# Four taps of q's convolution on VectorE, convolutions finished half by half, and ranks from a difference, in a MetaFormer block

## The reference, cut to what matters

```python
x = x + conv_attention(layernorm_over_channels(x))
t = tokens(x);  t = t + mixture_of_experts(layernorm(t));  return image(t)

# conv_attention, cut to its steps
qkv = einsum('bchw,oc->bohw', x, w_qkv) + b_qkv
qkv = max over 2x2 positions                     # 24 x 24 are left
qkv = 3x3 depthwise convolution(qkv, w_dw) + b_dw
q, k, v = split(qkv)                             # 8 heads of 12 channels
q, k = q / clip(norm(q), 1e-12), k / clip(norm(k), 1e-12)
attn = einsum('bhcn,bhdn->bhcd', q, k) * temperature
out = sum over kk in (6, 8, 9, 9) of a_i * (topk_softmax(attn, kk) @ v)
out = gelu(out), repeated 2x2;  return einsum(out, w_proj) + b_proj
```

## Time and profile before

| | us |
|---|---|
| median of 3 runs | 164.18 (162.23 to 167.53) |
| the profiled execution | 162.02 |
| its span, first to last instruction | 160.1 |
| TensorE busy | 141.9 (89% of the span) |
| VectorE busy | 126.3 (79%) |
| ScalarE busy | 83.9 (52%) |
| GpSimd busy | 70.6 (44%) |

### The profile page before, as it was taken

The page is one execution under the profiler, slowest core; times in us unless marked ns, Lnnn a source line. Parts: engine busy times, 40 slices in busy tenths (PEclk is TensorE's granted clock), DMA queues, the critical chain, the costliest instruction groups (busy, mean ns, idle before and its releaser), DMA issues.

```text
span 160.1 us, 2626 instructions
## 1 busy us (share of the span) xinstructions
PE 141.9 (89%) x812; PEld 120.1 (75%) x812; DVE 126.3 (79%) x321; ACT 83.9 (52%) x153; POOL 70.6 (44%) x63
## 2 busy tenths in 40 slices
PE   7918959999989898999799928999999999999970
PEld 2404839999979573878568917999999999999950
DVE  0999877999868398927734997499799989989982
ACT  3525795304063503666677630666576566676730
POOL 8999953692000000200000789064736736526461
PEclk9996999999999999999999996999999999999998
DMA  5799000000000000000000001001001001000101
GB/s 145 204 256 246 5 0 4 2 0 0 4 0 0 0 2 0 4 0 0 0 0 4 0 0 37 0 0 37 4 0 37 0 0 37 0 0 0 37 0 37
DMA packets 3749, 4.41 MB, mean 28 GB/s; under 512 B 1934, under 2 KB 3290, under 8 KB 3644
## 3 DMA queue, kind: packets, MB, share of 16 engines
q1 hardware_dynamic: 3338, 3.86, 9.6%
q10 hardware_dynamic: 402, 0.44, 0.8%
HBM read 3.42 MB, written 0.88 MB: 27 GB/s over the span
## 4 chain that ended last, share of the span: by engine, by line
PE 65%; DVE 21%; issue 5%; ACT 4%; DMA 2%; SPq 0%; DVEq 0%; ACTq 0%
PE psum L912 15%; PE psum L914 14%; PE psum L913 14%; PE psum L1076 3%; PE psum L954 3%; PE psum L949 3%; PE psum L950 3%; PE psum L1006 3%; DMA xT<-xt 2%; DVE xn_lo L624 2%; DVE yg L849 2%; DVE h_hi L636 2%; DVE stats L697 2%; PE psum L1049 2%; PE psum L887 1%
## 5 line engine op out<-in xcount | busy, mean ns | idle before, releaser
L425 POOL TENSOR_TENSOR xs<-xs,yg 96x384 f32<-96x384 f32 x23 | 31.3, 1360 | 51.2 <-DVE yg L852 26.8
L638 DVE TENSOR_TENSOR h_lo<-hf,h_hi 128x768 fp32r<-128x768 f32 x30 | 38.4, 1280 | 9.8 <-ACT hf L533 9.1
L912 PE MATMUL psum<-xn_hi,w_hi 97*128 (+1 forms) x72 | 29.2, 406 | 0.5 <-DVE xn_lo L624 0.5
L533 ACT ACTIVATE hf<-psum 128x768 f32<-128x768 f32 x30 | 24.3, 809 | 5.7 <-PE psum L914 5.6
L912 PE MATMUL psum<-h_hi,w_hi 128*96 128x384 f32 x60 | 20.9, 348 | 4.9 <-DVE yg L852 3.7
L913 PE MATMUL psum<-xn_hi,w_lo 97*128 (+1 forms) x72 | 24.7, 343 | 0.0
L914 PE MATMUL psum<-xn_lo,w_hi 97*128 (+1 forms) x72 | 24.6, 342 | 0.0
L419 POOL TENSOR_TENSOR xs<-xs,pr 96x384 f32<-96x384 f32 x6 | 8.8, 1467 | 28.4 <-DVE gs L683 28.4
L532 ACT ACTIVATE h_hi<-psum 128x768 fp32r<-128x768 f32 x14 | 11.4, 814 | 18.3 <-PE psum L914 18.3
L914 PE MATMUL psum<-h_lo,w_hi 128*96 128x384 f32 x60 | 20.5, 342 | 0.0
L913 PE MATMUL psum<-h_hi,w_lo 128*96 128x384 f32 x60 | 20.4, 340 | 0.0
(11 more groups left out here) (173 smaller groups left out, 281.4 us busy)
## 6 DMA issues: line engine op xcount, KB each, us to landing
xs<-x SPq DMA_DIRECT2D x1, 864.0 KB, 9.9
out<-xs SPq DMA_DIRECT2D x6, 144.0 KB, 1.9
w1s<-w SPq DMA_DIRECT2D x1, 576.0 KB
w2s<-w SPq DMA_DIRECT2D x1, 576.0 KB, 6.6
xT<-xt SPq DMA_DIRECT2D x1, 432.0 KB, 4.5
xT<-xt SPq DMA_DIRECT2D x1, 288.0 KB, 3.7
pars<-par ACTq DMA_DIRECT2D x1, 196.5 KB
cst<-consts ACTq DMA_DIRECT2D x1, 170.0 KB, 4.5
```

Source lines behind the costliest of these rows:

```text
L425: pool.tensor_tensor(cols(xs, c), cols(xs, c), cols(yg, e), ALU.add).then_inc(acc_done, 1)
L533: act.activation(cols(hf, p % 2, 2 * CH).rearrange("p (j n) -> p j n", n=CH), src, ACT.Gelu).then_inc(gelu_done, 1)
L638: dve.tensor_tensor(lo, h, hi.bitcast(F32), ALU.subtract).then_inc(h_split, 1)
L912: pe.matmul(o, w_hi, m_hi, start=start, stop=False)
```

## The change

Of q's nine taps, taps 0 to 3 move from TensorE to VectorE: there they are summed with the bias over all 576 positions into a new tile `qpart`. TensorE keeps taps 4 to 8, and VectorE adds its result to `qpart` half by half (which takes q out of PSUM, in place of ScalarE). The diagonals of taps 0 to 3 are no longer made, on ScalarE and on GpSimd. v's taps 0 to 6 follow q's; taps 7 and 8 stand inside the chain of k's norm. `conv` now issues all products of one half before those of the other. w2's high part is made by ScalarE before q's diagonals, and its low part by GpSimd before that of k's grid. The ranks come from a difference and a comparison with a table that holds 0, or minus the smallest normal number where equal scores must count, in place of a greater-than, an equality, a product with a table of ones, and an addition.

```diff
+Q_TAPS = 4
+KNORM_AT = 7
...
             for t in range(9):
                 low_diagonal(t)
-            for t in range(9):
+            for t in range(Q_TAPS, 9):
                 w = P_DW + t
                 pool.tensor_scalar(qd_lo[:, t * C:(t + 1) * C], ident[0:C, 0:C],
...
             low(w1_lo[:, :], w1s[:, :], w1_hi[:, :], w_split)
+            pool.wait_ge(w_high, 2)
+            low(w2_lo[:, :], w2s[:, :], w2_hi[:, :], w_split)
             pool.wait_ge(kp_split, 1)
             low(kp_lo[:, :], pooled[:, PAD * PAD:2 * PAD * PAD], kp_hi[:, :], kp_split)
-            pool.wait_ge(w_high, 2)
-            low(w2_lo[:, :], w2s[:, :], w2_hi[:, :], w_split)
             pool.wait_ge(qp_split, 1)
...
             take_high(0, 5)
-            for t in range(9):
+            act.wait_ge(w2_in, 16)
+            act.activation(w2_hi[:, :], w2s[:, :], ACT.Copy).then_inc(w_high, 1)
+            for t in range(Q_TAPS, 9):
...
-            for b in range(2):
-                act.wait_ge(qmm_done, b + 1)
-                act.activation(qkc[:, b * HP:(b + 1) * HP], bank(b, cols=HP), ACT.Identity,
-                               bias=pars[0:C, P_BDW:P_BDW + 1]).then_inc(qconv_done, 1)
...
+            def whole_tap(g, t, first, o, done):
+                w = pars[0:C, P_DW + 9 * g + t:P_DW + 9 * g + t + 1]
+                if first:
+                    return dve.tensor_scalar(grid(o), tap(g, t), w, pars[0:C, P_BDW + g:P_BDW + g + 1], ALU.mult,
+                                             ALU.add)
+                dve.wait_ge(done, t)
+                return dve.scalar_tensor_tensor(grid(o), tap(g, t), w, grid(o), ALU.mult, ALU.add)
+
+            for t in range(Q_TAPS):
+                whole_tap(0, t, t == 0, qpart[:, :], qtap_done).then_inc(qtap_done, 1)
+
+            def v_tap(t):
+                whole_tap(2, t, t == 0, vc[:, :], vtap_done).then_inc(vtap_done if t < 8 else v_ready, 1)
+
+            def v_beside(step):
+                if step % 2 == 0 and KNORM_AT + step // 2 < 9:
+                    v_tap(KNORM_AT + step // 2)
+
+            for t in range(KNORM_AT):
+                v_tap(t)
             dve.wait_ge(ssq_done, 1)
-            link(dve.tensor_scalar(n2[:, 1:2], ssq[:, 1:2], 1e-24, None, ALU.max))
-            rsqrt(rnorm[:, 1:2], n2[:, 1:2], n2h[:, 1:2], n2t[:, 1:2], n2u[:, 1:2]).then_inc(knorm_done, 1)
+            link(dve.tensor_scalar(n2[:, 1:2], ssq[:, 1:2], 1e-24, None, ALU.max), v_beside, 0)
+            rsqrt(rnorm[:, 1:2], n2[:, 1:2], n2h[:, 1:2], n2t[:, 1:2], n2u[:, 1:2], v_beside).then_inc(knorm_done, 1)
+            for t in range(KNORM_AT + 5, 9):
+                v_tap(t)
+            dve.wait_ge(qtap_done, Q_TAPS)
             for b in range(2):
+                dve.wait_ge(qmm_done, b + 1)
+                q = qkc[:, b * HP:(b + 1) * HP]
+                dve.tensor_tensor(q, bank(b, cols=HP), qpart[:, b * HP:(b + 1) * HP],
+                                  ALU.add).then_inc(qconv_done, 1)
                 dve.wait_ge(qconv_done, b + 1)
-                q = qkc[:, b * HP:(b + 1) * HP]
                 ins = dve.scalar_tensor_tensor(sqj[:, b * HP:(b + 1) * HP], q, 1.0, q, ALU.mult, ALU.mult,
...
-            dve.tensor_tensor(sq3(above), other, own, ALU.is_gt)
-            link(dve.tensor_tensor(sq3(equal), other, own, ALU.is_equal))
-            link(dve.tensor_tensor(equal[:, :], equal[:, :], cst[0:C, K_TRI:K_TRI + DH * DH], ALU.mult))
-            link(dve.tensor_tensor(above[:, :], above[:, :], equal[:, :], ALU.add))
+            link(dve.tensor_tensor(sq3(ahead), other, own, ALU.subtract))
+            link(dve.tensor_tensor(above[:, :], ahead[:, :], cst[0:C, K_TRI:K_TRI + DH * DH], ALU.is_gt))
             link(dve.tensor_reduce(rank[:, :], sq3(above), AX.X, ALU.add))
...
-            def conv(at, w_hi, w_lo, p_hi, p_lo, split, done):
+            def conv(at, taps, w_hi, w_lo, p_hi, p_lo, split, done):
...
-                pe.wait_ge(split, 2)
-                for b in range(2):
-                    for t in range(9):
+                    pe.wait_ge(split, 2)
+                    for t in taps:
                         ins = pe.matmul(bank(at + b, cols=HP), w_hi[:, t * C:(t + 1) * C], tap_of(t, p_lo, b),
                                         start=False, stop=(t == 8))
                     ins.then_inc(done, 1)
...
-            conv(4, diag_hi, diag_lo, kp_hi, kp_lo, kp_split, kconv_done)
+            conv(4, range(9), diag_hi, diag_lo, kp_hi, kp_lo, kp_split, kconv_done)
...
-            conv(0, qd_hi, qd_lo, qp_hi, qp_lo, qp_split, qmm_done)
+            conv(0, range(Q_TAPS, 9), qd_hi, qd_lo, qp_hi, qp_lo, qp_split, qmm_done)
```

More of the change, by code:

```diff
@@ L201, in build @@
         sqj = sb("sqj", [C, PIX])
+        qpart = sb("qpart", [C, PIX])
         ssq = sb("ssq", [C, 3])
@@ L213, in build @@
         above = sb("above", [C, DH * DH])
-        equal = sb("equal", [C, DH * DH])
+        ahead = sb("ahead", [C, DH * DH])
         rank = sb("rank", [C, DH])
@@ L266, in build @@
         qmm_done, qconv_done = sem("qmm_done"), sem("qconv_done")
-        vtap_done, v_ready = sem("vtap_done"), sem("v_ready")
+        vtap_done, v_ready, qtap_done = sem("vtap_done"), sem("v_ready"), sem("qtap_done")
         ssq_done, knorm_done, khat_ready = sem("ssq_done"), sem("knorm_done"), sem("khat_ready")
@@ L482, in _ @@
             act.activation(qp_hi[:, :], pooled[:, 0:PAD * PAD], ACT.Copy).then_inc(qp_split, 1)
-            act.wait_ge(w2_in, 16)
-            act.activation(w2_hi[:, :], w2s[:, :], ACT.Copy).then_inc(w_high, 1)
             for b in range(2):
@@ L942, in _ @@
                       cols(xn_lo, c)).then_inc(qkv_done, 1)
-            def conv(at, w_hi, w_lo, p_hi, p_lo, split, done):
+            def conv(at, taps, w_hi, w_lo, p_hi, p_lo, split, done):
                 for b in range(2):
-                    for t in range(9):
+                    for t in taps:
                         d = slice(t * C, (t + 1) * C)
-                        pe.matmul(bank(at + b, cols=HP), w_hi[:, d], tap_of(t, p_hi, b), start=(t == 0), stop=False)
+                        pe.matmul(bank(at + b, cols=HP), w_hi[:, d], tap_of(t, p_hi, b), start=(t == taps[0]),
+                                  stop=False)
                         pe.matmul(bank(at + b, cols=HP), w_lo[:, d], tap_of(t, p_hi, b), start=False, stop=False)
-                pe.wait_ge(split, 2)
-                for b in range(2):
-                    for t in range(9):
+                    pe.wait_ge(split, 2)
+                    for t in taps:
                         ins = pe.matmul(bank(at + b, cols=HP), w_hi[:, t * C:(t + 1) * C], tap_of(t, p_lo, b),
@@ L960, in _ @@
             pe.wait_ge(kp_split, 1)
-            conv(4, diag_hi, diag_lo, kp_hi, kp_lo, kp_split, kconv_done)
+            conv(4, range(9), diag_hi, diag_lo, kp_hi, kp_lo, kp_split, kconv_done)
             pe.wait_ge(pool_done, V_POOLED)
-            pe.wait_ge(qd_set, 18)
+            pe.wait_ge(qd_set, 2 * (9 - Q_TAPS))
             pe.wait_ge(qp_split, 1)
-            conv(0, qd_hi, qd_lo, qp_hi, qp_lo, qp_split, qmm_done)
+            conv(0, range(Q_TAPS, 9), qd_hi, qd_lo, qp_hi, qp_lo, qp_split, qmm_done)
             def turn(g, b):
@@ L1122, in _constants @@
     k[:C, K_CEN:K_CEN + C] = np.eye(C) - 1.0 / C
-    k[:, K_TRI:K_TRI + DH * DH] = np.tril(np.ones((DH, DH)), -1).reshape(-1)
+    k[:, K_TRI:K_TRI + DH * DH] = -np.finfo(np.float32).tiny * np.tril(np.ones((DH, DH)), -1).reshape(-1)
     return k
```

## The result

The changed kernel takes 173.44 us (median of 4 runs, 171.92 to 175.38), the kernel before 163.20 in the same comparison (162.21 to 167.53): a ratio of 1.062, 95% interval 1.044 to 1.079. It is slower by about 10 us, where 163.9 and no change were forecast, and outside the range. The profiled execution took 172.45 (span 170.7) against 162.02 (160.1).

What follows compares the result with a forecast made beforehand. VectorE, not TensorE, would now set the time, four added taps about offsetting the removed turns with GpSimd. Terms of -0.05 before the ranks and -0.26 from them gave -0.3: 164.18 to 163.9 us, range 161.8 to 166.0.

Steps and rivals of the forecast that it cites:

- the sum behind 163.9: Change in the start of the attention matrix's transpose, -0.05 - 0.26 = -0.3 us, carried to the end from 164.18.
- rival 1: TensorE's clock falls in the 3.2 us gap behind q's convolution, costing 1.3 us: 165.2; chance 0.35.
- the "108 us" behind the transpose: Stretch after the attention matrix's transpose, claimed to keep its length because the work there is the same.
- the 53.8: Sign of being wrong: the attention matrix's transpose starting before 51.5 or behind 53.8.
- T: Time of a first tap alone on VectorE, taken as 0.8 us, bounds 0.62 and 1.50; two such taps.
- k's chain: VectorE's chain of k's norm, with two of v's taps inside: 3.65 us long, ending at 44.2 against 43.90.
- q's norm: Start of q's norm on VectorE: forecast at 46.1 against 46.21 before.
- the two additions: VectorE's additions taking q out of PSUM half by half: about 0.45 us each, bounds 0.35 and 0.54.
- Rival 2: VectorE's first taps are slow, T = 1.4, everything behind 1.2 us later: 165.1; chance 0.13.
- Rival 3: VectorE's first taps are fast, two elements at a time, T = 0.41, gaining 0.8 us more: 163.1; chance 0.10.
- The turns with GpSimd: VectorE's early taps and GpSimd take turns; w2's new place removes these, some 3.5 us.
- The ranks: Shorter rank computation gains 0.54 us on VectorE; 0.26 counts at the transpose, 0.28 becomes waiting for TensorE.

Runs made afterwards that it cites:

- e2: Kernel before with q's convolution on TensorE cut to taps 4 to 8, the others computed nowhere and the gap left unfilled: 173.92 us, ratio 1.064.
- e6: Changed kernel with nine products of zeros in place of one ahead of the scores: 165.95 us.
- e5: Changed kernel with three products of zeros behind q's convolution: 171.49 us.
- e9: e4 with w2's high and low parts back at their old place and 16 idle products behind q's convolution: 167.30 us, ratio 1.014.
- e4: Changed kernel with three of q's taps on VectorE in place of four: 162.38 us, ratio 0.990.
- e12: e4 with the ranks made the old way, by four instructions: 161.03 us, ratio 0.985.
- e1: Changed kernel with ten products of zeros filling the gap behind q's convolution: 163.90 us, ratio 1.005.
- e11: Kernel before with 16 products of zeros in TensorE's first gap, ahead of the first transposes: 161.93 us, ratio 0.993.
- e10: Changed kernel with two of q's taps on VectorE and 16 products of zeros in TensorE's first gap: 160.63 us, ratio 0.982.

## Why the prediction was wrong

**The step that failed is the clock: the sum behind 163.9 has no term for it, and rival 1, which has one, priced it at 1.3 us and gave it a chance of 0.35.** Rival 1 had the place, the mechanism and the sign: the gap behind q's convolution, 0.50 granted between 44 and 50, the scores and the 18 products paying. The size was taken from the low stretches of the trace before, 3.4 us each (3.3 in the prediction). This one is 27.3 us, and the price about 10. Two things were missed. What the two rows have in common was not looked at: behind them stand products of 384 columns or idle ones of 512, and the clock came back while these ran. Behind this gap stand 72 instructions of 100 columns and 25 of 96, with only four of 288 and two idle ones of 512 among them. At half clock they kept TensorE busy and the clock stayed low (here and in e2); at full clock they ran and it stayed up (e6, and the kernel before from 47 to 59). It came back at 70.9, behind line 1023's products of 288 columns and during the idle ones of line 901. And the price was charged only up to the transpose, where 4.7 us had been lost; the 18 products behind it (line 1020) ran at half clock as well, and the "108 us" behind the transpose, which were to keep their length, grew by 5.9. The transpose at 57.24 is also beyond the 53.8 that the prediction named as its sign of being wrong.

The Trainium skill says that a stretch of sustained matmuls releases the clock (TensorE: Matmul & The Clock Gate, "What's actually happening"); here 25.13 busy us of 26.00 did not, and the measurement decides.

**Its chance** was set to 0.35 because the gap would be 3.2 us, shorter than the two of 3.7 where the clock had fallen. It was 2.3, shorter still, and the clock fell in the profiled run, and by the mean clocks of 0.867 to 0.898 in all four. With 1.45 us of gap it still fell in three of four (e5). The 12 transposes between the gap and the scores did not save it.

**VectorE's taps.** T was taken as 0.8 with bounds 0.62 and 1.50. v's tap 0, with GpSimd idle, took 0.57, below the low bound, and q's 0.85 beside GpSimd's memset. k's chain ended at 43.59 against a forecast of 44.2: about 0.2 by the two first taps, and 0.4 because the chain with two of v's taps inside took 3.25 and not 3.65. q's norm started at 45.37 against 46.1, and the two additions took 0.45 each, as forecast. Rival 2 falls. Rival 3's number is nearest, with 0.57 for its 0.41; whether its mechanism (two elements at a time) is the reason, no run shows.

**The turns with GpSimd**, read from two long instructions and two GpSimd rows, held in kind and size: 3.5 read, 3.4 measured (e9 against e4). So w2's new place is what makes room for q's taps.

**The ranks.** Forecast: 0.26 of 0.54 reaches the end, the rest is VectorE waiting for TensorE. Measured with three taps: nothing of it reaches the end (e12). With four taps and the clock held (e1) the attention matrix was done at 52.73 and the transpose started at 53.27, so there too VectorE waited for the whole 0.54.

**The sum.** With the clock held the stretch from the first tap to the transpose was 1.3 us shorter (e1), where 0.3 was forecast: the scores came 1.1 earlier, which the prediction had at nothing, and 0.25 came behind them. The time of e1 doesn't show it, since it lost 2.1 in its trace to a longer first low stretch. That run-to-run scatter was put into the range as noise and not asked for its cause, which is largely the same clock (e11).

## What to carry to other kernels

Before work is taken off TensorE, look at what follows the hole that it leaves. In this kernel small products followed, the low clock lasted as long as they did, and a hole of 2.3 us cost 10. So look first at what ran when the clock came back elsewhere in the trace, and only then at how long the hole is. Two ways out worked here: balance the split so that no large hole opens (three or two taps in place of four), or put products of zeros into the hole before the clock falls, which cost nothing there. Neither is a guarantee, since the clock also fell behind shorter gaps in some executions (below).

## What the runs showed of the hardware

- The same 36 instructions of 100 columns took 4.19 us at the full clock and 7.89 at half, and the clock kept either level while they ran: the full one in e6 from 51.1 to 63, the half one in e2 from 45 to 74.
- During nine idle products of 512 columns the clock came back 3.4 us after it had fallen (e6, low only from 47.7 to 51.1).
- With a gap of 0.6 us none of the ten runs of e4 had a mean clock under 0.933, where the falls in the changed kernel gave 0.867 to 0.898; a gap of 1.45 us brought the clock down in three runs of four (e5).
- Shorter gaps can do it too, and long products don't always bring it back at once. The profiled run of e10 was at half clock from 23.3 to 30.2, behind waits on VectorE of 0.85, 0.33 and 0.56 us, and from 23.9 it ran products of 384 columns without a break, 6.3 us of them at half clock. The kernel before has the same three waits (0.86, 0.33, 0.56) and kept the full clock in its trace. By their mean clocks (0.963 against 0.980 and 0.981) no other run of e10 fell there (163.52 against 160.51 to 160.64). Its window:

```profile
23.20:31.00 7.80, 7.24 (x25) 0.56 0.00 0
```
